# One learning step of a memory layer, reordered: half of a projection held back, slopes, statistics and a halving moved

## The chip, the core and the metric

The program runs on one core of one Trainium2 chip, as one launch. The metric is device time in microseconds (us) of that core; lower is better. The engines are named as in the profile: PE is TensorE (PEld its weight loads), DVE VectorE, ACT ScalarE, POOL GpSimd, SP SyncE, which here only issues DMAs. Each engine runs its own instructions in program order and waits on semaphores for the others.

## What is computed

A two-layer block: a test-time memory and a feed-forward part on layer 0, then attention and a routed mixture of experts on layer 1. The change touches only the first part of the first, the learning of the memory on x (16 sequences of 512 positions, width 128, layer-normalised). It is cut into 8 chunks of 64 positions, and the chunks are learned one after the other:

```
k = rmsnorm(silu(xc @ wk.T), k_norm);  v = silu(xc @ wv.T)
def mem_fwd((w0, w1, ln), k):                      # w0: 256x128, w1: 128x256, ln: 128
    return k + rmsnorm(silu(k @ w0.T) @ w1.T, ln)
def step((mem, surp), (k_c, v_c, th_c, eta_c, beta_c)):
    grads = grad(mean((v_c - mem_fwd(mem, k_c)) ** 2 * th_c))
    clip  = min(1 / (norm(grads) + 1e-6), 1)
    surp  = eta_c * surp - grads * clip
    mem   = beta_c * mem + surp
```

The gates th, eta and beta (1 - alpha) come from sums over the normalised x of the same chunk. Each step needs the memory that the step before it left.

## The kernel before, in words

`learn` holds the learning. A chunk is 1024 rows of 128, that is 8 tiles (`CT`) of 128 x 128, worked on in two halves of 4 tiles (`HT`), h = 0 and h = 1. Every engine has a hand-written list of calls for each step s in 0 to 7; there is no scheduler. The order in the lists and the semaphores alone decide what runs when.

In step s the memory's own work is: PE `hidden` (k @ w0, L437), ACT its tanh (`m_tz`, L629), DVE the silu product (`m_hid`, L858), PE `transpose_h` (L451), ACT `copy_ht` (L637), PE `output` (L461), ACT the squares (L645) and DVE their sums (L868), POOL a power (`m_r`, L768), ACT `normalise_y` (`m_nrm`, L651), and then, for each half, DVE `errors` (L874, L876), `derivatives` (L881 to L890) and `remainder` (L895). `derivatives` contains the dot product over the row (`m_dot`, L888) and its scaled form `m_dr` (L889), for which ACT's `along_y` (L657) waits; `remainder` subtracts what `along_y` wrote and gives `m_dy`. PE transposes `m_dy` (`transpose_dy`, L469), ACT copies it (`copy_dyt`, L667), PE makes the gradients: `grad_hidden` (L478), `grad_w1` (L491), `grad_ln` (L487, which reads `m_en`) and `grad_w0` (L498, after DVE's `grad_hidden`, L904). `norm` (L505 to L508) and DVE's `update` (L908 to L918) end the step.

`slope` (DVE, L862) is the factor tanh - 1 times hidden - 2 that DVE's `grad_hidden` reads. `keep_surprise` (ACT, L663) scales the old surprise; DVE's `decayed` (L899) reads it.

Between these stands work on later chunks. For s + 1: `weigh_keys`, `gates`, `transpose_k` (L406), `copy_kt` (L611), `halve_v` (ACT, L598: v times 0.5), `subtract_v` (POOL). For s + 2: `project` (PE, L397: 4 tiles times wk and 4 times wv for each half, h = 1 first; half 0 waits for `copy_kt`), `project_tanh` (ACT, L587), `silu` (DVE, L836), `square_k` (ACT, L592), `scale_k` (ACT, L603), `sum_products` (L847). For s + 3: `normalise_x` (ACT, L567), transposes and copies of x. For s + 4: `statistics` (DVE, L825 and L830). SP loads a chunk of x (`m_xin`, L352) into the buffer that `normalise_x` of two chunks before has done with. Where no such chunk is left (steps 6 and 7 have no s + 2) the calls drop out.

## Time and profile before

| | |
|---|---|
| time, median of 3 runs | 3584.17 us (3581.29 to 3584.71) |
| the profiled execution: its own time, its span | 3609.93 us, 3608.1 us |
| prologue of the learning | 0 to 51.6 us of the span |
| steps 0 to 7 and what closes the stage | 51.6 to 383.2 us |
| everything behind it, untouched by the change | 383.2 to 3608.1 us |
| busy in the span: PE, DVE, ACT, POOL | 90%, 71%, 58%, 23% |

A step is counted from the start of PE's `hidden` (L437). In step 2 that is 134.34 us of the span, in step 3 175.31 us. Since steps 1 to 4 repeat each other to within 0.01 us, one of them is enough to read.

### The profile page before, as it was taken

To read this page: it belongs to the slowest core of one execution; us is meant where nothing else is said; L and a number is where in the kernel's file an instruction comes from. 1 tells how busy PE (TensorE), PEld (TensorE's weight loads), DVE (VectorE), ACT (ScalarE), POOL (GpSimd) and SP (SyncE) were. 2 spreads that over 40 slices of the span, in tenths; PEclk is the share of its full clock that TensorE was granted. 3 is DMA by queue.
4 is the path that set the end of the run, shared out by engine and by line. 5 is a ranking of instruction groups with operands and counts; after the bars stand their busy time and mean duration, and the time that the engine had idled before them with its cause. 6 is when DMAs were issued, how large, how long until landed. Compare 5 with 4: busy or idle time off the path is not lost. (4 is left out here: it accounts for less than half of the span.)

```text
span 3608.1 us, 77385 instructions
## 1 busy us (share of the span) xinstructions
PE 3255.2 (90%) x30347; PEld 1894.3 (53%) x30347; DVE 2575.5 (71%) x5104; ACT 2079.1 (58%) x4212; POOL 838.7 (23%) x753
## 2 busy tenths in 40 slices
PE   6887599999999699999999999769999999999998
PEld 5776322222222277777777777535555444444454
DVE  5776688888888266676666776577777777777774
ACT  6664177777777544434334333226667776777766
POOL 3331111101110132422423323133333121112110
PEclk8998699999999899999999999879999999999999
DMA  4100211111110000110110110032222112111101
GB/s 137 30 13 1 54 51 49 42 54 46 54 51 28 27 18 28 32 34 22 32 34 22 32 34 22 28 82 57 59 59 49 50 50 67 38 47 42 54 26 29
DMA packets 180473, 151.89 MB, mean 42 GB/s; under 512 B 44388, under 2 KB 160900, under 8 KB 179972
## 3 DMA queue, kind: packets, MB, share of 16 engines
q1 hardware_dynamic: 172228, 140.43, 13.8%
q0 software_dynamic: 6144, 4.72, 1.0%
q8 instruction: 257, 4.21, 0.5%
q10 hardware_dynamic: 1728, 1.57, 0.2%
q14 instruction: 116, 0.95, 0.1%
HBM read 48.45 MB, written 32.65 MB: 22 GB/s over the span
## 5 line engine op out<-in xcount | busy, mean ns | idle before, releaser
L1395 DVE TENSOR_REDUCE b_maxima<-psum 128x2 f32<-128x1024 f32 (+3 forms) x768 | 774.2, 1044 | 236.9 <-PE psum L1227 209.8
L1333 ACT ACTIVATE b_prob<-psum 128x512 f32<-128x512 f32 (+2 forms) x1536 | 725.5, 526 | 332.6 <-PE psum L1260 313.1
L1395 DVE TENSOR_REDUCE c_maxima<-psum 128x2 f32<-128x1024 f32 x512 | 602.6, 1221 | 119.3 <-PE psum L1221 118.2
L1333 ACT ACTIVATE c_prob<-psum 128x512 f32<-128x512 f32 x1024 | 535.9, 602 | 186.7 <-PE psum L1253 186.3
L1860 PEld LDWEIGHTS psum<-consts_layer,a_hid 128*128 128x128 f32 x4096 | 476.2, 192 | 53.6 <-issue 53.3
L1860 PE MATMUL psum<-consts_layer,a_hid 128*128 128x128 f32 x4096 | 477.8, 274 | 0.0
L1850 PE MATMUL psum<-a_x1t,consts_layer 128*128 128x512 f32 x1024 | 461.2, 596 | 11.6 <-issue 11.3
L1917 ACT ACTIVATE a_hid<-psum,consts_layer 128x512 f32<-128x512 f32 x512 | 347.9, 687 | 208.0 <-PE psum L1850 201.1
L1253 PE MATMUL psum<-b_qa,b_ka 64*128 64x512 bf16 (+3 forms) x2048 | 365.5, 303 | 60.8 <-ACT b_prob L1333 56.6
L1275 PE MATMUL psum<-b_prob,b_v 128*32 128x512 f32 (+3 forms) x4096 | 386.8, 450 | 0.3
L2062 DVE SCALAR_TENSOR_TENSOR a_acc<-psum,a_gprob,a_acc 128x128 f32<-128x128 f32 x512 | 143.8, 343 | 266.7 <-PE psum L1860 253.4
L1253 PE MATMUL psum<-c_qa,c_ka 64*128 64x512 bf16 x1024 | 271.0, 382 | 63.9 <-ACT c_prob L1333 62.4
L1221 PE MATMUL psum<-b_ka,b_qa 62*128 62x512 bf16 (+3 forms) x2048 | 300.1, 307 | 27.3 <-DMA b_ka<-b_part 13.2
L1850 PEld LDWEIGHTS psum<-a_x1t,consts_layer 128*128 128x128 f32 x1024 | 187.9, 191 | 213.1 <-issue 204.2
L1253 PEld LDWEIGHTS psum<-b_qa,b_ka 64*128 64x128 bf16 x2048 | 123.0, 93 | 297.5 <-ACT b_prob L1333 223.9
L1275 PE MATMUL psum<-c_prob,c_v 128*32 128x512 f32 x2048 | 272.7, 605 | 0.1
L1260 PE MATMUL psum<-b_kmask,b_pick 64*128 64x64 bf16 x4096 | 253.0, 191 | 0.0
L1221 PE MATMUL psum<-c_ka,c_qa 62*128 62x512 bf16 x1024 | 202.0, 392 | 27.4 <-DMA c_ka<-c_part 13.8
L1227 PE MATMUL psum<-b_qmask,b_pick 64*128 64x64 bf16 x4096 | 221.1, 191 | 3.3 <-issue 3.3
L1227 PEld LDWEIGHTS psum<-b_qmask,b_pick 64*128 64x128 bf16 x4096 | 194.4, 97 | 54.4 <-issue 7.3
L1260 PEld LDWEIGHTS psum<-b_kmask,b_pick 64*128 64x128 bf16 x4096 | 184.8, 95 | 47.3 <-issue 1.7
L1946 POOL TENSOR_TENSOR a_share<-a_gprob,consts_layer 128x512 f32<-128x512 f32 x128 | 134.1, 1048 | 273.2 <-DVE a_gprob L2001 264.4
(343 smaller groups left out, 4303.2 us busy)
## 6 DMA issues: line engine op xcount, KB each, us to landing
b_qa<-b_part SPq DMA_DIRECT2D x192, 128.0 KB
c_qa<-c_part SPq DMA_DIRECT2D x96, 128.0 KB, 2.5
c_ka<-c_part SPq DMA_DIRECT2D x90, 128.0 KB, 2.5
b_ka<-b_part SPq DMA_DIRECT2D x90, 128.0 KB
consts_layer<-layer_in SPq DMA_DIRECT2D x1, 5419.0 KB, 19.2
m_xin<-x SPq DMA_DIRECT2D x16, 256.0 KB, 4.2
xnt<-m_xt SPq DMA_DIRECT2D x16, 256.0 KB, 2.7
c_xt<-xnt SPq DMA_DIRECT2D x16, 256.0 KB, 2.8
```

Of the source, the lines that this page charges most:

```text
L1221: last = nc.tensor.matmul(out[:, half, k0:k0 + w], qa[rows, hh, t * P:(t + 1) * P], ka[rows, hh, 0:w], start=True, stop=not self.causal)
L1227: last = nc.tensor.matmul(out[:, half, k1:k1 + HALF], self.pick[n][rows, :], self.qmask[rows, :], start=False, stop=n == 1)
L1253: last = nc.tensor.matmul(outs[half][:, k0:k0 + w], ka[rows, hh, t * P:(t + 1) * P], qa[rows, hh, q0:S], start=True, stop=not self.causal)
L1260: last = nc.tensor.matmul(outs[half][:, k0 + n * HALF:k0 + (n + 1) * HALF], self.pick[n][rows, :], self.kmask[rows, :], start=False, stop= ...
L1275: last = nc.tensor.matmul(self.acc[32 * j:32 * (j + 1), q0:S], self.values(p)[:, t, column:column + 32], self.prob[:, s % 2, j, q0:S], sta ...
L1333: self.nc.scalar.activation(out, src, ACT.Exp, scale=SCALE).then_inc(self.s.free, 1)
L1395: self.nc.vector.reduce_max(out, src, X).then_inc(self.m.free, 1)
L1850: nc.tensor.matmul(bank[4 + u % 3], K("up0", e * F0 + f * P, P), x1t[n][:, :], start=True, stop=True).then_inc(up_ready.sem, 1)
L1860: last = nc.tensor.matmul(tiled(2 + e % 2)[:, t, :], hid[:, e % 2, f, t * P:(t + 1) * P], K("down0", (e * FC + f) * D, D), start=f == 0, s ...
L1917: nc.scalar.activation(hid[:, e % 2, f, :], bank[4 + u % 3], ACT.Relu, bias=K("upb0", u, 1)).then_inc(hid_ready.sem, 1)
L1946: own.done(nc.gpsimd.tensor_tensor(share[k % 2][:, :, :], along(gprob[n][:, :, k], D), over(K("downb0", k * D, D), T), ALU.mult))
L2062: last = nc.vector.scalar_tensor_tensor(acc[n][:, t, :], tiled(2 + e % 2)[:, t, :], gprob[n][:, t, e:e + 1], acc[n][:, t, :], ALU.mult, AL ...
```

## The change

On PE, `project(s + 2)` is split. Its half 1 stays where it was; its half 0 goes behind `grad_ln(s, 0)` and waits for `m_dr` of half 0. `grad_w1(s, 0)` goes ahead of `grad_hidden(s, 0)`. On DVE, `remainder(s, 0)` goes ahead of `errors(s, 1)`; `slope` leaves the sums of squares: half 0 goes ahead of them, half 1 to between the two halves of `grad_hidden`; `sum_products` goes behind both; `statistics` is cut in two, `sums` (8 BN_STATS) at the head of the step and `moments` (8 BN_AGGR) behind `gates`. On ACT, `halve_v` is gone: the 128 x 128 weight wv is halved once, at the very start (`halve_wv`), and `project_tanh` takes v with scale 1.0; `copy_kt` goes ahead of `normalise_y(s, 1)`, `keep_surprise` behind `along_y(s, 0)`, `square_k(s + 2, 1)` ahead of `along_y(s, 1)`, `normalise_x` is in one piece behind `copy_dyt(s, 1)`, and `scale_k` is in two halves around `copy_xs` and `gate_tanh`. POOL's `subtract_v` waits for `silu` where it waited for `halve_v`.

```diff
@@ project, on PE
                     for h in halves:
+                        pe.wait_ge(wv_halved.sem, 1)
                         pe.wait_ge(xt_copied.sem, xt_copied.at(n, h + 1))
@@ the step's list on PE
                     if has(s + 2):
-                        project(s + 2)
+                        project(s + 2, (1,))
                     grad_ln(s, 0)
+                    if has(s + 2):
+
+                        pe.wait_ge(dr_ready.sem, dr_ready.at(s, 1))
+                        project(s + 2, (0,))
                     transpose_dy(s, 0)
+                    grad_w1(s, 0)
                     grad_hidden(s, 0)
-                    grad_w1(s, 0)
                     grad_ln(s, 1)
@@ new on ACT in place of halve_v
-                def halve_v(n):
-                    act.wait_ge(silu_ready.sem, silu_ready.at(n, 4))
-                    nc.scalar.activation(tv[n % 2][:, :, :], tv[n % 2][:, :, :], ACT.Copy, scale=0.5).then_inc(vn_ready.sem, 1)
+                def halve_wv():
+                    act.wait_ge(consts, 32)
+                    nc.scalar.activation(K("wv"), K("wv"), ACT.Copy, scale=0.5).then_inc(wv_halved.sem, 1)
@@ the step's list on ACT
                     normalise_y(s, 0)
-                    keep_surprise(s)
-                    normalise_y(s, 1)
                     if has(s + 1):
                         copy_kt(s + 1)
+                    normalise_y(s, 1)
                     if has(s + 2):
                         project_tanh(s + 2, (1,))
                     along_y(s, 0)
+                    keep_surprise(s)
                     if has(s + 2):
                         project_tanh(s + 2, (0,))
                     copy_dyt(s, 0)
-                    if has(s + 3):
-                        normalise_x(s + 3, (0,))
-                    if has(s + 1):
-                        halve_v(s + 1)
+                    if has(s + 2):
+                        square_k(s + 2, 1)
                     along_y(s, 1)
                     copy_dyt(s, 1)
                     if has(s + 3):
-                        normalise_x(s + 3, (1,))
+                        normalise_x(s + 3)
                     if has(s + 2):
-                        square_k(s + 2, 1)
                         square_k(s + 2, 0)
@@ the step's list on DVE
+                    if has(s + 4):
+                        sums(s + 4)
                     for h in range(2):
                         hidden(s, h)
                     if has(s + 1):
                         weigh_keys(s + 1)
                         gates(s + 1)
+                    if has(s + 4):
+                        moments(s + 4)
+                    slope(s, 0)
                     output_deviations(s)
                     errors(s, 0)
                     derivatives(s, 0)
                     if has(s + 2):
                         silu(s + 2, 1)
+                    remainder(s, 0)
                     errors(s, 1)
-                    remainder(s, 0)
                     derivatives(s, 1)
                     decayed(s)
                     remainder(s, 1)
                     if has(s + 2):
                         silu(s + 2, 0)
                     grad_hidden(s, 0)
+                    slope(s, 1)
+                    grad_hidden(s, 1)
                     if has(s + 2):
                         sum_products(s + 2)
-                    grad_hidden(s, 1)
-                    if has(s + 4):
-                        statistics(s + 4)
                     update(s)
```

PE's queue in one step, between the transposes of the keys and `grad_w0`, before the change (m_xt is the projection, m_en `grad_ln`, m_dy with m_hid `grad_w1`, m_dyt `grad_hidden`):

```order
L406 MATMUL psum<-consts_shared,m_kn 128x128 x8
L397 MATMUL psum<-consts_memory,m_xt 128x128 x16
L487 MATMUL psum<-m_en,m_ths 128x128 x4
L469 MATMUL psum<-consts_shared,m_dy 128x128 x4
L478 MATMUL psum<-mem,m_dyt 128x256 x4
L491 MATMUL psum<-m_hid,m_dy 128x256 x4
L487 MATMUL psum<-m_en,m_ths 128x128 x4
L469 MATMUL psum<-consts_shared,m_dy 128x128 x4
```

The same place with the change:

```order
L407 MATMUL psum<-consts_shared,m_kn 128x128 x8
L398 MATMUL psum<-consts_memory,m_xt 128x128 x8
L488 MATMUL psum<-m_en,m_ths 128x128 x4
L398 MATMUL psum<-consts_memory,m_xt 128x128 x8
L470 MATMUL psum<-consts_shared,m_dy 128x128 x4
L492 MATMUL psum<-m_hid,m_dy 128x256 x4
L479 MATMUL psum<-mem,m_dyt 128x256 x4
L488 MATMUL psum<-m_en,m_ths 128x128 x4
```

Eight of the sixteen projection products now stand directly ahead of the transposes of the first `m_dy`, and `grad_w1` ahead of `grad_hidden`. DVE's queue behind the first `derivatives`, before (m_tk, m_tv are `silu`, m_m `errors`, m_dy `remainder`):

```order
L890 TENSOR_TENSOR m_dn<-m_dn,m_rth 128x512
L836 SCALAR_TENSOR_TENSOR m_tk<-m_tk,psum 128x512
L836 SCALAR_TENSOR_TENSOR m_tv<-m_tv,psum 128x512
L874 TENSOR_TENSOR m_m<-m_nrm,mem 128x512
L876 TENSOR_TENSOR m_m<-m_m,m_kv 128x512
L895 TENSOR_TENSOR m_dy<-m_dn,m_p 128x512
L881 TENSOR_TENSOR m_en<-m_m,m_nrm 128x512
```

And with the change:

```order
L897 TENSOR_TENSOR m_dn<-m_dn,m_rth 128x512
L844 SCALAR_TENSOR_TENSOR m_tk<-m_tk,psum 128x512
L844 SCALAR_TENSOR_TENSOR m_tv<-m_tv,psum 128x512
L902 TENSOR_TENSOR m_dy<-m_dn,m_p 128x512
L881 TENSOR_TENSOR m_m<-m_nrm,mem 128x512
L883 TENSOR_TENSOR m_m<-m_m,m_kv 128x512
L888 TENSOR_TENSOR m_en<-m_m,m_nrm 128x512
```

The first `m_dy` comes two instructions earlier; everything from L888 on stands at the same count. ACT's queue from the first `copy_dyt` to the second, before (m_tk, m_tv ahead of it are `project_tanh`):

```order
L587 ACTIVATE m_tv<-psum 128x512
L667 ACTIVATE m_dyt<-psum 128x512
L567 ACTIVATE m_xn<-m_xin,m_shift,m_rstd 128x128 x4
L598 ACTIVATE m_tv<-m_tv 128x1024
L657 ACTIVATE m_p<-m_nrm,m_dr 128x128 x4
```

And with the change:

```order
L589 ACTIVATE m_tv<-psum 128x512
L671 ACTIVATE m_dyt<-psum 128x512
L594 ACTIVATE m_sq,m_ks<-m_tk 128x128 x4
L661 ACTIVATE m_p<-m_nrm,m_dr 128x128 x4
L671 ACTIVATE m_dyt<-psum 128x512
L570 ACTIVATE m_xn<-m_xin,m_shift,m_rstd 128x128 x8
```

Ahead of the second `along_y` four squares stand where four normalisations and the halving stood.

## Rows read from the trace of the kernel before

**Rows 1.** Behind the learning: length, PE, PEld, DVE, ACT, POOL busy, clock, DMA, GB/s

```profile
383.20:3608.10 3224.90, 2963.86 (x28649) 1633.74 (x28649) 2329.05 (x4582) 1850.40 (x3578) 731.91 (x651) 0.97 0.16 42
```

**Rows 2.** The same view of steps 0 and 2

```profile
51.63:93.36 41.73, 34.07 (x212) 30.46 (x213) 30.75 (x74) 27.69 (x77) 12.36 (x12) 0.92 0.09 21
...
134.34:175.31 40.97, 34.99 (x215) 31.45 (x214) 30.56 (x66) 28.20 (x80) 13.28 (x12) 0.92 0.11 27
```

**Rows 3.** Timeline of step 2, PE and PEld: start, duration, line, idle before, releaser

```profile
141.51 3.71 PEld L461 LDWEIGHTS psum<-memw1t,m_ht 128*128 128x128 f32 x32 [0.22 <-ACT m_ht L637]
...
146.12 1.95 PE L397 MATMUL psum<-consts_memory,m_xt 128*128 128x128 f32 x16
...
151.30 3.16 PE L397 MATMUL psum<-consts_memory,m_xt 128*128 128x128 f32 x16 [3.23 <-ACT m_kt L611]
...
156.84 0.66 PE L469 MATMUL psum<-consts_shared,m_dy 128*128 128x128 f32 x4 [0.99 <-DVE m_dy L895]
...
158.18 3.23 PE L478 MATMUL psum<-mem,m_dyt 128*128 128x256 f32 x8 [0.69 <-ACT m_dyt L667]
...
163.42 1.05 PE L487 MATMUL psum<-m_en,m_ths 128*128 128x128 f32 x8
...
164.31 0.60 PE L469 MATMUL psum<-consts_shared,m_dy 128*128 128x128 f32 x4
...
164.75 1.89 PE L491 MATMUL psum<-m_hid,m_dy 128*128 128x256 f32 x8
...
166.48 1.89 PE L478 MATMUL psum<-mem,m_dyt 128*128 128x256 f32 x8
...
175.31 3.70 PE L437 MATMUL psum<-mem,m_kt 128*128 128x256 f32 x16
```

**Rows 4.** Timeline of step 2, DVE

```profile
138.02 2.35 DVE L858 SCALAR_TENSOR_TENSOR m_hid<-m_tz,psum 128x1024 f32<-128x1024 f32 x2 [2.67 <-ACT m_tz L629]
...
148.47 0.69 DVE L874 TENSOR_TENSOR m_m<-m_nrm,mem 128x512 f32<-128x512 f32 x1 [1.27 <-ACT m_nrm L651]
...
152.65 0.16 DVE L889 TENSOR_TENSOR m_dr<-m_dot,m_rth 128x4 f32<-128x4 f32 x1
...
154.65 0.68 DVE L874 TENSOR_TENSOR m_m<-m_nrm,mem 128x512 f32<-128x512 f32 x1
...
156.09 0.69 DVE L895 TENSOR_TENSOR m_dy<-m_dn,m_p 128x512 f32<-128x512 f32 x1
...
159.41 0.16 DVE L889 TENSOR_TENSOR m_dr<-m_dot,m_rth 128x4 f32<-128x4 f32 x1
...
160.22 0.89 DVE L899 SCALAR_TENSOR_TENSOR m_base<-mem,m_eb,m_keep 128x640 f32<-128x640 f32 x1
...
161.80 0.69 DVE L895 TENSOR_TENSOR m_dy<-m_dn,m_p 128x512 f32<-128x512 f32 x1 [0.70 <-ACT m_p L657]
...
169.54 1.64 DVE L825 BATCH_NORM_STATS2 m_stats<-m_xin 128x6 f32<-128x128 f32 x8
```

**Rows 5.** Timeline of step 2, ACT

```profile
136.98 2.12 ACT L629 ACTIVATE m_tz<-psum 128x1024 f32<-128x1024 f32 x2
...
159.56 1.04 ACT L598 ACTIVATE m_tv<-m_tv 128x1024 f32<-128x1024 f32 x1
```

**Rows 6.** PE in four stretches of step 2: length, busy, granted clock (1.00 is full speed)

```profile
138.04:141.51 3.47, 2.40 (x20) 1.00 0.00 0
151.95:155.35 3.40, 3.40 (x19) 0.50 0.00 0
155.35:158.75 3.40, 1.73 (x11) 1.00 0.00 0
158.75:162.15 3.40, 3.40 (x10) 0.50 0.02 5
```

**Rows 7.** Timeline of step 6, ACT, without a projection

```profile
317.69 1.28 ACT L657 ACTIVATE m_p<-m_nrm,m_dr 128x128 f32<-128x128 f32 x4 [1.69 <-DVE m_dr L889]
```

**Rows 8.** Loads of x (L352), all 16: issue to landing

```profile
DMA to landing us min/median/max: 3.6/4.2/8.4
```

More of the change, by code:

```diff
@@ L557, in _, with normalise_x @@
             def _(act):
-                def normalise_x(n, halves=(0, 1)):
-                    if 0 in halves:
-                        act.wait_ge(rstd_ready.sem, rstd_ready.at(n, 1))
-                    if 0 in halves and n > 0:
+                def normalise_x(n):
+                    act.wait_ge(rstd_ready.sem, rstd_ready.at(n, 1))
+                    if n > 0:
                         act.wait_ge(xt_ready.sem, xt_ready.at(n, 0))
@@ L564, in normalise_x @@
                         act.wait_ge(prod_ready.sem, prod_ready.at(n - 1, 1))
[L565 to L569 removed]
+                    for t in range(CT):
+                        last = nc.scalar.activation(xn[:, t, :], xin[n % 2][:, t, :], ACT.Identity, bias=shift[:, t:t + 1], scale=rstd[:, t:t + 1])
+                    last.then_inc(xn_ready.sem, 1)
                 def copy_xt(n, h):
@@ L687, in _ @@
                     square_k(0, h)
-                halve_v(0)
                 for h in range(2):
@@ L739, in _ @@
                             copy_xt(s + 3, h)
+                    if has(s + 2):
+                        scale_k(s + 2, (0,))
+                    if has(s + 3):
                         copy_xs(s + 3)
@@ L742, in _ @@
                         gate_tanh(s + 2)
-                        scale_k(s + 2)
+                        scale_k(s + 2, (1,))
                 copy_w1t(NC)
@@ L826, in statistics, with moments @@
                     own.done(last)
+                def moments(n):
                     if n > 0:
```

39 lines of the change are left out of this document (21 added, 18 removed).

## The prediction

> **What bounds the kernel now.** First the windows by stage: 3224.9 us of the span lie behind the learning [rows 1], and no line of the change is there; whatever it brings must come out of the eight steps. The windows by step show that a step takes 40.97 us with PE busy for 34.99 us, and that the mean granted clock is 0.92 [rows 2]. No engine is full, so I read one step, step 2, engine by engine in the timeline, and looked in each for the wait that ends last.
>
> PE's rows [rows 3] are read from the end. From the transposes of the second `m_dy` (L469) at 164.31 us to the next step's `hidden` at 175.31 us PE's list runs through without a wait that matters: 11.00 us, a tail of fixed length. Ahead of it PE has also been busy since 158.18 us. The last real waits are 0.69 us for `copy_dyt` at 158.18 us and 0.99 us for the first `m_dy` at 156.84 us. So the step is as long as the first `m_dy` is late, plus what PE has queued behind it. That queue is also slower than it need be. `grad_hidden` and `grad_w1`, 8 rows each, take 5.24 us together (158.18 to 163.42), where at full clock each takes 1.73 us (164.75 to 166.48). The windows say why: the granted clock is 0.50, that is 1.2 GHz in place of 2.4, from 151.95 to 155.35 us and again from 158.75 to 162.15 us, each time behind a stretch in which PE had waited, with 3.23 us of idle before 151.30 us and with 1.73 us of work in 3.40 before the second [rows 3, 6].
>
> DVE's rows [rows 4] show the other chain. DVE has no wait between 148.47 us, the first `errors`, and 161.1 us, the end of `decayed`; then it waits 0.70 us for ACT's `along_y`, which ACT could start only behind `halve_v`, at 160.60 us [rows 5], though `m_dr` had been ready since 159.57 us. The second `m_dy` is done at 162.49 us. PE reaches its transposes only at 164.31 us, so today PE's queue decides, by 1.8 us.
>
> **The change, part by part, in the times of step 2.**
>
> *Head of the step.* The tanh of the first half starts at 136.98 us [rows 5], while half of the 3.70 us of `hidden` after 134.34 us is done by about 136.3 us: ACT was in `scale_k`. Half of `scale_k` now comes before `copy_xs`, in time in which ACT waited for PE, so the tanh comes about 0.6 us sooner. PE however has the transposes of the other half to do first; what reaches `output` is the 0.22 us for which it waited for `copy_ht` [rows 3]. I take 0.2 us, and move all later times by it. The 8 BN_STATS, 1.64 us, now stand ahead of DVE's `hidden`. DVE waited there for 2.67 us, 2.1 us with the earlier tanh [rows 4]; they fit with 0.45 us over, and cost nothing as long as their x has landed (third rival). The aggregates and `slope` of half 0 fall where DVE waited for squares of y. Leaving the tail they save nothing, since DVE waited for `norm` anyway. The halving of wv is one 128 x 128 operation, hidden under the first load and POOL's powers: nothing.
>
> *First `m_dy`.* `remainder` goes ahead of two `errors` operations of 0.72 us. It may start when the silu products end, 154.65 - 0.2 = 154.45 us; its `along_y` has started at `m_dr` (152.81 - 0.2 + 0.1) and takes 1.28 us [rows 7], so it is ready at 154.0 us. `m_dy` is done at 155.15 us, where it was 156.78 us: 1.6 us sooner.
>
> *The held half.* It starts at `m_dr`, about 152.7 us. Where it stood before, it had 151.30 to 154.46 us; it takes 1.95 us at full clock (146.12 us) and 3.16 us at half [rows 3]. It is on PE's path now, since it stands ahead of the transposes. Behind it PE has the transposes (164.31 to 164.75, 0.44 us), `grad_w1` and `grad_hidden` (1.73 us each) and `grad_ln` (163.42 to 164.31, 0.89 us), with no wait, as `grad_w1` needs no copy and gives `copy_dyt` its time. 152.7 + 1.95 + 0.44 + 1.73 + 1.73 + 0.89 = 159.45 us at full clock. A half-speed stretch of 3.4 us, as both in rows 6 are, adds 1.7 us: one gives 161.15 us, two that lie wholly on this piece 162.85 us. I expect one always, because PE still idles for some 2.5 us before the first `grad_ln`, and part of a second now and then.
>
> *Second `m_dy`.* DVE's count of instructions to it is the same, so 161.1 - 0.2 = 160.9 us for the end of `decayed`. `along_y` can start at 159.57 - 0.2 = 159.4 us: ahead of it now stand four squares, which are done before, and ends at 160.75 us. The wait of 0.70 us is gone; `m_dy` is done at 160.9 + 0.69 = 161.6 us, its transposes can start at 161.65 us.
>
> *Sum of a step.* The tail starts at the later of PE's and DVE's times: 161.65 us with up to one half-speed stretch, 162.85 us with two, against 164.31 us. Gains of 2.66 and 1.46 us; I take 2.3 us, nearer to DVE's end, because the second stretch rarely lies wholly there. What is late next is DVE. The tail stays 11.00 us if ACT keeps up: `copy_dyt`, the whole normalisation of x, four squares and the squares of the gradients come to 6.5 us there, and `grad_w0` ends 7.5 us after the tail's start. `slope` of half 1, 1.2 us, lies where DVE waits for PE's second `grad_hidden`. Cover gone, it would cost those 1.2 us.
>
> *All steps.* Six steps (0 to 5) have a projection: 6 x 2.3 = 13.8 us. Step 0 was 41.73 us long, 0.76 us more than step 2 [rows 2], which I take to be more slow PE work in the same piece, gone with it: 0.8 us more. Steps 6 and 7 have no silu products to cover `along_y`: DVE waits about 0.7 us in front of `remainder`, but still gives the first `m_dy` 1.44 - 0.7 = 0.7 us sooner, and PE is what counts there: 0.7 us each, 1.4 us. Together 16.0 us. The profiled execution took 3609.93 us, 0.7% above the median of the runs; the terms are the same few microseconds in either: 3609.93 - 16.0 = 3593.9 us, and 3584.17 - 16.0 = 3568.2 us.
>
> **Rivals.**
>
> *The clock gives it back.* The split leaves PE one more gap, between the first `grad_ln` and the held half, and a wait of up to 1.2 us for the second `m_dy`. If each step gets two full half-speed stretches or a new one in the tail, its gain is 1.2 to 1.46 us. For it: today each step has two. Against it: from 152.7 us on PE has work nearly without a break. 6 x 1.3 + 0.8 + 0 = 8.6 us: 3575.6 us.
> The Trainium skill ("TensorE: Matmul & The Clock Gate", "A second HAM failure mode") says that short idles between groups of matmuls can make the clock go back and forth between its two levels; by that rule this case holds. Its "Part 4: PE-mode transpose" says that transposes do not count as busy in the same way, which would make the first `m_dy`'s transposes a gap too. The trace does not bear that out: between 138.04 and 141.51 us PE did hardly anything but transposes of `m_hid`, and the clock stayed at 1.00 [rows 6].
>
> *A queue on ACT eats most of it.* The second tanh of the held half stands ahead of `copy_dyt`, four squares and the second `along_y`. With the projection at half clock its last tanh ends at 156.5 us, `copy_dyt` at 157.3 us, the squares at 158.5 us; `along_y` is due at 159.4 us. If the 0.9 us of room is not there and 1.3 us more are lost on top, a gain of 1 us a step is left: 3578 us, about the edge of no change.
>
> *Slower, by the load of x.* BN_STATS stands at the head of DVE's queue, with the silu products of the hidden layer behind it, PE's transposes behind them, and so the whole step. Its x is loaded into the buffer that `normalise_x` frees, and this now ends in one piece at about 166.3 us. With 1.3 us for two issues and 4.2 us to land it is there at 171.8 us, some 2.1 us before DVE asks for it. The longest load took 8.4 us [rows 8]: late by 2.1 us, of which 0.45 us is covered. It turns a step's gain into a loss above 4.2 + 2.1 + 0.45 + 2.3 = 9 us. Were loads to take 11 us, each of steps 0 to 3 would lose 2 us and the rest gain little: about 3592 us. No load in the trace took so long.
>
> **How the numbers follow.** Forecast 0.61, the clock 0.20, ACT's queue 0.13, the load 0.06. 0.2% of this kernel is 7.2 us, about what a measurement can tell from no change. The first two are faster by more than that, and a little of the third: 0.83; same 0.12; slower 0.05. The best that the bounds allow is 6 x 2.66 + 0.8 + 2 x 1.4 (the 0.69 us before `grad_hidden` also gone in steps 6 and 7) = 19.6 us, 3564.6 us; less the runs' own spread of some 3 us, and as much again for a clock that comes out better, 3560 us. The upper end takes in the clock's case and ends at ACT's: 3578 us.
>
> **What would show it.** In the changed profile: steps of some 38.7 us; the first `m_dy` about 20.8 us after `hidden`, the second about 27.3 us; DVE without a wait before the second `remainder`; PE without one between the held half and `grad_ln`, then at most a short one for the second `m_dy`; mean clock of a step above 0.92. I am wrong if DVE waits for x at BN_STATS, if the distance from the second transposes to the next `hidden` is more than 11.0 us, or if PE shows two stretches at 0.50 between the held half and them.

## The result and the profile after

| | before | after |
|---|---|---|
| time, median (lowest to highest) | 3584.44 us (3581.29 to 3585.27), 4 runs | 3556.83 us (3555.72 to 3559.12), 4 runs |
| ratio, 95% interval | | 0.9925 (0.9908 to 0.9943) |
| profiled execution: own time, span | 3609.93 us, 3608.1 us | 3559.12 us, 3557.3 us |
| start of step 0, end of the last w1 transposes | 51.63, 381.88 us | 50.62, 353.43 us |

The change takes 27.6 us off, where 16.0 were forecast: the right direction, and a gain 1.7 times as large. The two profiled spans lie 50.8 us apart. Only 28.45 us of that are in the learning. The other 22.35 us lie behind it, in work that is the same in both kernels (3226.22 and 3203.87 us). That part belongs to the execution that was profiled, which for the kernel before took 25 us more than the median. In the later profiles it took 3220 to 3225 us on one chip and 3198 to 3207 us on two others, with the change or without it. So only the learning is compared here.

The windows by step of the changed kernel, each from the start of `hidden` (now L438) to the next; the first is the prologue. Columns as in [rows 2]:

```profile
0.00:50.62 50.62, 24.72 (x152) 23.96 (x153) 18.46 (x70) 28.11 (x90) 20.48 (x28) 0.87 0.76 233
50.62:87.75 37.13, 31.59 (x213) 28.62 (x213) 30.62 (x75) 28.03 (x80) 11.32 (x12) 1.00 0.10 24
...
124.88:162.01 37.13, 31.60 (x214) 28.62 (x214) 30.40 (x66) 27.46 (x79) 12.24 (x12) 1.00 0.12 29
...
199.15:236.99 37.84, 34.14 (x215) 31.28 (x214) 28.41 (x50) 27.70 (x79) 12.23 (x12) 0.91 0.06 15
236.99:274.23 37.24, 31.68 (x191) 28.79 (x190) 28.01 (x49) 24.67 (x74) 10.15 (x8) 0.90 0.03 7
274.23:313.34 39.11, 30.03 (x153) 26.03 (x153) 25.04 (x45) 16.25 (x37) 4.93 (x4) 0.83 0.00 0
313.34:353.43 40.09, 28.33 (x145) 24.80 (x145) 24.64 (x44) 15.39 (x35) 2.58 (x3) 0.81 0.00 1
```

Steps were 41.73, 40.98, 40.97, 40.97, 40.97, 40.52, 41.33 and 42.78 us long and are now 37.13, 37.13, 37.13, 37.14, 37.84, 37.24, 39.11 and 40.09 us: 27.4 us less in all. In steps 0 to 3 the mean granted clock is 1.00; it was 0.92 [rows 2]. PE's busy time fell with it, 34.99 to 31.60 us, for the same products (215 and 214 records). DVE's busy time is what it was (30.56 and 30.40 us).

It is tempting to stop at that clock: the steps became short when the half-speed stretches went. But step 4 is at clock 0.91, with 34.14 us of busy PE, and is only 0.7 us longer than step 3. So a slow clock as such does not make a step 3.8 us longer; it depends on what the slow stretch lies on, as the experiments show. PE in step 2, in the timeline, from the projection to the second `m_dy`:

```profile
136.33 1.95 PE L398 MATMUL psum<-consts_memory,m_xt 128*128 128x128 f32 x16
139.88 1.16 PE L488 MATMUL psum<-m_en,m_ths 128*128 128x128 f32 x8 [1.60 <-DVE m_en L888]
142.07 2.05 PE L398 MATMUL psum<-consts_memory,m_xt 128*128 128x128 f32 x16 [1.04 <-DVE m_dr L896]
144.60 0.66 PE L470 MATMUL psum<-consts_shared,m_dy 128*128 128x128 f32 x4 [0.47 <-DVE m_dy L902]
145.09 1.89 PE L492 MATMUL psum<-m_hid,m_dy 128*128 128x256 f32 x8
146.82 1.89 PE L479 MATMUL psum<-mem,m_dyt 128*128 128x256 f32 x8
148.54 1.05 PE L488 MATMUL psum<-m_en,m_ths 128*128 128x128 f32 x8
150.96 0.66 PE L470 MATMUL psum<-consts_shared,m_dy 128*128 128x128 f32 x4 [1.36 <-DVE m_dy L902]
```

Every wait that is left is for DVE, the last of them 1.36 us long. Before, PE came to the second transposes without a wait [rows 3]. The bound has gone over to DVE's chain, and what counts is when that chain starts and how long it is. Its start, in the rows of POOL, ACT and DVE of the same step. POOL's `m_r` is the inverse root with which y is normalised, a power over 128 x 4 elements, once for each half:

```profile
135.22 0.17 DVE L876 TENSOR_SCALAR m_ss<-m_ss 128x4 f32<-128x4 f32 x1
135.47 1.01 POOL L772 TENSOR_TENSOR m_r<-m_ss,m_power 128x4 f32<-128x4 f32 x1 [4.80 <-DVE m_ss L876]
136.51 1.14 ACT L655 ACTIVATE m_nrm<-psum,m_r 128x128 f32<-128x128 f32 x4 [0.26 <-POOL m_r L772]
137.68 0.69 DVE L881 TENSOR_TENSOR m_m<-m_nrm,mem 128x512 f32<-128x512 f32 x1 [0.51 <-ACT m_nrm L655]
...
150.22 0.68 DVE L902 TENSOR_TENSOR m_dy<-m_dn,m_p 128x512 f32<-128x512 f32 x1
```

The same place in the kernel before:

```profile
144.95 0.17 DVE L869 TENSOR_SCALAR m_ss<-m_ss 128x4 f32<-128x4 f32 x1
145.17 1.22 DVE L862 SCALAR_TENSOR_TENSOR m_dz<-m_tz,m_dz 128x1024 f32<-128x1024 f32 x1
145.20 3.08 POOL L768 TENSOR_TENSOR m_r<-m_ss,m_power 128x4 f32<-128x4 f32 x2 [5.08 <-DVE m_ss L869]
```

And the source line's view of POOL's power over all 16 instructions, before and then after (shortest, median and longest in ns):

```profile
L768 POOL TENSOR_TENSOR m_r<-m_ss,m_power x16: 1006/1508/2079, 62.2 to 353.4; 128x4 f32<-128x4 f32 x16
```

```profile
L772 POOL TENSOR_TENSOR m_r<-m_ss,m_power x16: 1006/1009/1019, 61.2 to 327.4; 128x4 f32<-128x4 f32 x16
```

Before, two powers in a row took 3.08 us: 2.08 and 1.01. Now each takes 1.01 us. It is the first of each step that has become 1.07 us shorter, and in the kernel before DVE ran `slope` of half 1 beside it, 1.22 us, which reads two operands in SBUF. The change moved that `slope`. The first `errors` starts 12.80 us after `hidden` (137.68 - 124.88), where it started 14.13 us after it (148.47 - 134.34, [rows 4]), and DVE has no wait from there to the second `m_dy`. Of the 1.33 us, 1.07 are the power; the other 0.26 were there before it, since the first sum of squares ends about that much earlier after `hidden`, close to the 0.2 us that the prediction took for the earlier tanh.

### The profile page after: what moved, and what is told of

Its sections match the earlier page's. It is cut to its first block and busy times, and to the rows that moved or that the text cites. A ratio compares the mean times of both kernels' runs of the same rounds, so it can differ in the third digit from the quotient of the medians.

```text
span 3557.3 us, 77385 instructions
## 1 busy us (share of the span) xinstructions
PE 3228.3 (91%) x30347; PEld 1876.0 (53%) x30347; DVE 2573.2 (72%) x5104; ACT 2074.8 (58%) x4205; POOL 830.2 (23%) x753
## 5 line engine op out<-in xcount | busy, mean ns | idle before, releaser
L1236 PE MATMUL psum<-c_ka,c_qa 62*128 62x512 bf16 x1024 | 201.2, 391 | 27.4 <-DMA c_ka<-c_part 13.6
```

The costliest lines, as they stand in the source:

```text
L1236: last = nc.tensor.matmul(out[:, half, k0:k0 + w], qa[rows, hh, t * P:(t + 1) * P], ka[rows, hh, 0:w], start=True, stop=not self.causal)
```

## The experiments

Three theories of the part that the prediction missed. The lock (L in the expectations): a DVE operation with two inputs in SBUF holds up POOL's power beside it, and moving it away starts DVE's chain 1.07 us sooner in each of the eight steps. The clock: the steps became shorter since PE no longer drops to half speed, which the held half of the projection brings. The order: `remainder` and `grad_w1` put forward bring more than the sum gave them. The times of the kernel before differed between the chips (3605.68 us for the first four kernels, 3584.36 for the next four, 3584.03 for the last four), so each kernel is given as a ratio to the kernel before beside it. Steps are those of the profiled execution, steps 0 to 7.

**`slope` of half 1 moved alone, in the kernel before.**

```diff
                     for h in range(2):
-                        slope(s, h)
+                        if h == 0:
+                            slope(s, 0)
                         dve.wait_ge(y_squared ...
...
+                    slope(s, 1)
                     grad_hidden(s, 1)
```

> The kernel before with one edit: slope of half 1 leaves the place between the two sums of squares and goes between the two grad_hidden of DVE. Theory L (POOL's power of half 0 is held while DVE's slope, with both inputs in SBUF, runs beside it): the first power takes 1.0 us in place of 2.08 us, and since the first m_dy comes 1.1 us sooner and PE decides, every step is 1.1 us shorter: 8.5 us in all, 3576 us. Rival C (only the clock and the order on PE brought the time): the power's length is an artefact of the trace, the step stays at 40.97 us, 3584 us.

Ratio 0.9990 (0.9980 to 1.0000), 3602.57 us. POOL's first power fell to 1.01 us as expected, the time hardly at all. The ten runs lie between 3590.69 and 3608.79 us, and the profiled one, with 3594.41 us, is among the fastest. Its steps are 39.45, 38.83, 39.71, 38.81, 39.70, 37.79, 39.97 and 42.23 us long, with one half-speed stretch ahead of the second `m_dy` in each of steps 0 to 5, where steps 1 to 5 of the kernel before have two: 16.8 us after `hidden` in the shorter ones and 22.3 us in the longer. In both kinds the first `m_dy` comes 1.06 us earlier after `hidden` and PE reaches the second transposes without a wait, so in this execution PE's queue decides, and steps 1 to 4 are 2.2 and 1.3 us shorter. The median moved by 3.1 us of the 8.5 that were expected, the interval reaches from 0 to 7 us, and no trace shows what took the rest in the other nine runs. The move of `slope` alone is worth little; whether it is worth something behind the other edits is the next kernel's question.

**`slope` of half 1 put back, in the changed kernel.**

```diff
                     for h in range(2):
+                        if h == 1:
+                            slope(s, 1)
                         dve.wait_ge(y_squared ...
...
                     grad_hidden(s, 0)
-                    slope(s, 1)
                     grad_hidden(s, 1)
```

> The changed kernel with slope of half 1 put back between the two sums of squares. Theory L: first power back to 2.1 us, first normalisation 1.1 us later, DVE's chain to the second m_dy with it: steps of 38.2 us in place of 37.13 us, 9 us in all, 3566 us. Rival C: less than 2 us, 3558 us. If PE's later start also brings a stretch at half clock back, up to 1.7 us more in some steps: up to 3573 us.

Ratio 0.9943 (0.9927 to 0.9960), 3585.92 us. At the changed kernel's ratio it would be 0.9925 x 3605.68 = 3578.6 us, so putting it back costs 7.3 us, with intervals that overlap. The next kernel, which has `slope` in its new place and the time of the changed kernel, ran on the same chip: all its runs (3575.55 to 3580.19 us) lie below all of these (3581.95 to 3592.39), 8.5 us in the medians. The profile is sharper. POOL's power, and the first `errors` of step 1:

```profile
L772 POOL TENSOR_TENSOR m_r<-m_ss,m_power x16: 1006/1508/2077, 63.5 to 335.5; 128x4 f32<-128x4 f32 x16
...
105.00 0.69 DVE L883 TENSOR_TENSOR m_m<-m_nrm,mem 128x512 f32<-128x512 f32 x1 [1.28 <-ACT m_nrm L655]
```

The same 2.08 us as in the kernel before, and `errors` starts 13.86 us after `hidden` (105.00 - 91.14) in place of 12.80. The steps are 39.88, 38.21, 38.85, 38.21, 38.21, 37.75, 39.00 and 41.29 us. Steps 1 and 3 are 38.21 - 37.13 = 1.08 us and 1.07 us longer: the power's 1.07 us. All eight together are 8.6 us longer, but not by 1.08 us each: step 0, with a half-speed stretch on `hidden`, is 2.75 us longer, step 4 is 0.37 us longer and step 6 0.1 us shorter, as the half-speed stretches fall otherwise in the two profiles. That the sum is eight times the power's price is partly luck. The price itself is shown.

**The projection not held: whole, at its old place.**

```diff
-                        project(s + 2, (1,))
+                        project(s + 2)
                     grad_ln(s, 0)
-                    if has(s + 2):
-                        pe.wait_ge(dr_ready.sem, dr_ready.at(s, 1))
-                        project(s + 2, (0,))
```

> The changed kernel with the whole projection in its old place, behind copy_kt, and without the wait for m_dr. PE then works through both halves and the first grad_ln and has some 3 us of nothing before the first m_dy. Theory C (the hold pays by keeping PE busy, and the clock up, in front of the gradients): granted clock 0.50 in a stretch behind that gap in steps 0 to 5; where it falls on grad_w1 and grad_hidden they end about 1.8 us later, of which the wait of 1.4 us for the second m_dy covers most: 0.4 us a step, 3559 to 3562 us, with the mean clock of a step near 0.92. Rival (the hold pays by its order): no drop of the clock and no change, 3557 us.

Ratio 0.9923 (0.9906 to 0.9939), 3577.41 us: that of the changed kernel. The steps are 38.75, 37.15, 37.16, 37.24, 37.24, 36.80, 38.19 and 39.64 us. Each of steps 1 to 5 has a half-speed stretch now. Step 0, step 2 and the stretch in step 2, in the windows:

```profile
51.58:90.33 38.75, 32.91 (x212) 29.71 (x213) 30.62 (x74) 28.14 (x80) 11.30 (x12) 0.96 0.10 23
...
127.48:164.64 37.16, 32.69 (x215) 29.80 (x214) 30.44 (x66) 27.48 (x79) 12.24 (x12) 0.95 0.12 29
147.00:150.40 3.40, 3.19 (x10) 2.75 (x11) 3.33 (x7) 2.38 (x11) 0.00 (x0) 0.50 0.02 5
```

In step 2 the clock is 0.95 against 1.00, PE is busy for 1.1 us more, and the step is as long as in the changed kernel to 0.03 us. The stretch lies on `grad_w1`, and the 1.37 us for which PE otherwise waits for the second `m_dy` cover it. Step 0 shows the other case. Its stretch lies at the very start, on `hidden`, which takes 5.31 us in place of 3.70, and the step is 1.6 us longer: there nothing covers it. The holding of the projection, the edit by which the change is named, keeps the clock up in steps 1 to 3 and brings nothing here that the time shows. The clock theory falls for steps 1 to 5, not for every place in a step.

**PE kept busy in the kernel before.** `fill(n)` is n products of the identity with itself, 128 x 128, whose result nobody reads; nothing is left out.

```diff
-                        project(s + 2)
+                        project(s + 2, (1,))
+                        fill(10)
+                        project(s + 2, (0,))
                     grad_ln(s, 0)
+                        fill(3)
                     transpose_dy(s, 0)
+                        fill(2)
                     grad_hidden(s, 0)
```

> The kernel before with idle time of PE filled: 10 products of 128 x 128 with no use before the second half of the projection, 3 behind the first grad_ln, 2 behind the transposes of the first m_dy, in steps 0 to 5. Theory C: the granted clock stays at 1.00, grad_hidden and grad_w1 take 3.5 us in place of 5.24 us, a step is 1.8 us shorter: 10.7 us in all, 3573.5 us. Rival: the filling itself delays what stands behind it by as much as the clock gives, 3584 us.

Ratio 0.9991 (0.9982 to 1.0001), steps 1 to 4 of 40.65 to 40.92 us. The filling took away the first half-speed stretch and left the second, 23.2 to 27.2 us after `hidden`, ahead of the second `m_dy`. So it did not make the kernel that it was meant to make. It says only that without the first stretch, and with the filling, steps 1 to 4 are 0.05 to 0.33 us shorter.

**`remainder(s, 0)` back behind `errors(s, 1)`, in the changed kernel.**

```diff
-                    remainder(s, 0)
                     errors(s, 1)
+                    remainder(s, 0)
```

> The changed kernel with the first remainder back behind the second errors. The first m_dy comes 1.4 us later, DVE's count of instructions to the second is the same. Theory D (since the power is free of the lock, DVE's chain to the second m_dy sets the step, and PE has room of about 1.3 us before it): at full clock PE is ready at 150.9 us of step 2 where DVE's m_dy is due at 150.96 us, so the step stays at 37.2 us; where a stretch at half clock falls on this piece it is up to 1.7 us longer. Total 3 to 8 us over the changed kernel, which by its ratio is 3578.6 us on this chip: 3580 to 3587 us. Rival P (PE's queue from the first m_dy still sets the step): 1.4 us in every step, 11 us, 3590 us.

Ratio 0.9961 (0.9947 to 0.9975), 3569.63 us; 12.2 us slower than the changed kernel at its ratio. That is more than the 3 to 8 us expected and near the rival's 11. The profiled execution, with 3562.86 us the fastest of the five, does not bear out the rival's way, 1.4 us in every step; its steps are 38.68, 37.16, 38.69, 37.15, 37.16, 36.70, 38.00 and 40.26 us. Two windows, of a short and of a long one:

```profile
89.20:126.36 37.16, 32.88 (x214) 29.87 (x214) 30.43 (x66) 27.62 (x79) 12.28 (x12) 0.95 0.12 29
126.36:165.05 38.69, 33.06 (x214) 29.79 (x214) 30.16 (x65) 27.51 (x79) 12.25 (x12) 0.96 0.12 28
```

Both have one half-speed stretch, and the clock's mean is if anything better in the long step. It is the place that differs: 17.6 to 21.1 us after `hidden` in the short one, on the held half of the projection, where it comes out of PE's wait for the first `m_dy` (0.57 us of 1.93 are left), and 21.5 to 24.9 us in the long one, on `grad_w1` itself. In the timeline of the long one PE waits 1.93 us for that `m_dy` and then takes 3.38 us for what took 1.89:

```profile
147.54 0.89 PE L470 MATMUL psum<-consts_shared,m_dy 128*128 128x128 f32 x4 [1.93 <-DVE m_dy L902]
148.22 3.38 PE L492 MATMUL psum<-m_hid,m_dy 128*128 128x256 f32 x8
```

What the early `remainder` buys is room on PE: 1.36 us of wait for the second `m_dy`, into which such a stretch can fall. With the late one that room is gone (PE comes to the second transposes at 154.06 us in this step, without a wait), and a stretch behind the first `m_dy` lengthens the step by 1.5 us. Eight such steps would make the 12.2 us, but the profiled learning is only 1.0 us longer than the changed kernel's (303.80 and 302.81 us). That the slower four runs have more long steps is argued, not shown.

**`grad_hidden` ahead of `grad_w1` again, in the changed kernel.**

```diff
                     transpose_dy(s, 0)
-                    grad_w1(s, 0)
                     grad_hidden(s, 0)
+                    grad_w1(s, 0)
```

> The changed kernel with grad_hidden ahead of grad_w1 for the first half, as before the change, so that PE waits about 0.9 us for copy_dyt. Theory D: within PE's room, step 37.13 us unchanged at full clock, at most 3 us in all, 3579 to 3582 us. Rival P: 0.7 to 0.9 us a step, 6 us, 3585 us.

Ratio 0.9938 (0.9921 to 0.9955), 3559.86 us, steps of 37.04 to 37.45 us up to step 5 and 40.35 and 42.27 us in the last two, which were 39.11 and 40.09. In step 1 PE's wait for the second `m_dy` is 0.42 us where it was 1.36: the old order uses up room on PE and takes no time there. At the changed kernel's ratio it would be 3557.5 us: a difference of 2.4 us, which the intervals do not tell from none.

**`halve_v` back on ACT ahead of `along_y(s, 1)` and in the prologue.** The computation is that of the changed kernel, with v instead of wv halved.

```diff
                         square_k(s + 2, 1)
+                    if has(s + 1):
+                        halve_v(s + 1)
                     along_y(s, 1)
```

> The changed kernel with halve_v back: in the prologue behind the squares, in each step ahead of the second along_y (1.04 us on ACT); wv is copied onto itself with scale 1.0. In the step ACT has waited there for m_dr for 1.8 us, so the halving is free: steps of 37.13 us. In the prologue I expect the 1.0 us back by which the first hidden comes sooner with the change (50.62 for 51.63 us). In all 1 us, 3579.6 us. Rival (ACT's queue ahead of along_y is what the removal of halve_v freed): 0.7 us a step and more, 3584 us.

Ratio 0.9921 (0.9904 to 0.9939), 3555.70 us: no difference. Steps 0 to 3 are 37.14, 37.14, 37.72 and 37.15 us. Behind the squares and a halving of 1.05 us ACT still waits 0.83 us for `m_dr` before `along_y` (step 1). Step 0 starts at 51.81 us, where it started at 50.62 us; the last kernel below shows what that is worth.

**Three kinds of DVE operation beside POOL's power.** In the changed kernel DVE gets one more operation at the place that `slope` had: in steps 0 and 4 a product of two tiles in SBUF, in 1 and 5 a sum over one tile, in 2 and 6 a copy of one tile, in 3 and 7 nothing. The results are not read. The kernel ran once, 3564.89 us, and only its trace is used.

```diff
+                    if s % 4 == 0:
+                        nc.vector.tensor_tensor(scr[:, :, :], tz[:, part(0), :], tz[:, part(1), :], ALU.mult)
+                    elif s % 4 == 1:
+                        nc.vector.tensor_reduce(scs[:, :], tz[:, part(1), :], X, ALU.add)
+                    elif s % 4 == 2:
+                        nc.vector.tensor_copy(scr[:, :, :], tz[:, part(1), :])
```

> The changed kernel with an extra operation of DVE, whose result nobody reads, in the old place of slope of half 1, beside POOL's first power: in steps 0 and 4 a product of two SBUF inputs (1.2 us), in 1 and 5 a sum over one SBUF input, in 2 and 6 a copy of one SBUF input, in 3 and 7 none. The length of POOL's first power tells what holds it. Theory L (two inputs in SBUF hold it): 2.1 us in steps 0 and 4, 1.0 us in the others. Rival A (any long operation of DVE on SBUF does): 2.0 us in 1 and 5 too. Rival B (the power is longer for another reason, such as its own place behind slope): 1.0 us everywhere.

POOL's power in steps 0, 1, 2 and 3, and in the first three DVE's operation beside it, in the timeline:

```profile
62.18 1.22 DVE L876 TENSOR_TENSOR m_scr<-m_tz 128x1024 f32<-128x1024 f32 x1
62.35 2.93 POOL L774 TENSOR_TENSOR m_r<-m_ss,m_power 128x4 f32<-128x4 f32 x2 [5.88 <-DVE m_ss L888]
...
100.23 1.22 DVE L878 TENSOR_REDUCE m_scs<-m_tz 128x4 f32<-128x1024 f32 x1
100.40 1.01 POOL L774 TENSOR_TENSOR m_r<-m_ss,m_power 128x4 f32<-128x4 f32 x1 [4.80 <-DVE m_ss L888]
...
137.38 0.69 DVE L880 COPY m_scr<-m_tz 128x1024 f32<-128x1024 f32 x1
137.55 1.38 POOL L774 TENSOR_TENSOR m_r<-m_ss,m_power 128x4 f32<-128x4 f32 x1 [4.80 <-DVE m_ss L888]
...
175.07 1.01 POOL L774 TENSOR_TENSOR m_r<-m_ss,m_power 128x4 f32<-128x4 f32 x1 [4.54 <-DVE m_ss L888]
```

Of the same length, 1.22 us, the operation with two inputs adds 0.91 us to the first power (2.93 less the second's 1.01 is 1.92) and the one with one input nothing. So it is not that DVE is busy, nor that both read SBUF. The copy, with one input, adds 0.37 us, which no theory on record had. The ends say how the hold works: the power is done 0.87 us behind the end of the product (62.35 + 1.92 against 62.18 + 1.22), 0.86 us behind the end of the copy (138.93 against 138.07) and, in the kernel before, 0.89 us behind the end of `slope` (147.28 against 146.39). It gets on only when DVE's operation is over, whatever that one's length. The steps follow: 38.03, 37.16, 37.51 and 37.15 us, that is 0.90, 0.03, 0.38 and 0.02 more than 37.13. Steps 0 and 2 also have a half-speed stretch, but the time is lost ahead of it: the first `errors` starts 13.69, 12.81, 13.17 and 12.80 us after `hidden`. Steps 4 to 7, with the same four kinds, show the powers again (1.91, 1.02, 1.32 and 1.01 us). The Trainium skill ("SBUF — State Buffer", "🔬 SBUF: two separate sides") says that VectorE and GpSimd share a port pair under an exclusive lock, which a VectorE operation takes with two SBUF inputs or in a 2-port mode, and that a plain fp32 copy from SBUF to SBUF runs in that mode; the loser waits for the whole instruction. This case's rows agree on all three operations: 0.91, 0 and 0.37 us.

**The two swaps alone, in the kernel before.**

```diff
+                    remainder(s, 0)
                     errors(s, 1)
-                    remainder(s, 0)
...
+                    grad_w1(s, 0)
                     grad_hidden(s, 0)
-                    grad_w1(s, 0)
```

> The kernel before with two swaps and nothing else: the first remainder ahead of the second errors on DVE, and grad_w1 ahead of grad_hidden on PE for the first half. Theory P then D: PE gets from the first m_dy to its second transposes 1.4 us + 0.7 us sooner and stops deciding; DVE's chain, with the power still held by slope, decides: second transposes about 27.4 us after hidden, or 28.1 us if the wait for halve_v stays, steps of 38.4 to 39.1 us in place of 40.97 us. Over the stage 13 to 18 us less than before: a ratio of 0.995 to 0.9965. Rival (without the hold PE stays late, since the projection and the first grad_ln run at half clock in front of the first m_dy): steps above 40 us, less than 6 us.

Ratio 0.9956 (0.9938 to 0.9975), 3565.88 us. Steps of 38.20, 38.47, 38.47, 38.47, 38.47, 38.02, 39.67 and 40.63 us, steps 1 to 4 2.50 us shorter than before. Steps 1, 2 and 4 have a half-speed stretch, step 3 has none, and they are equally long: DVE decides. Two swapped pairs of calls bring 18.2 us, of the 26.3 that the whole change brings on the same chip (3584.03 to 3557.71 us), with the projection whole, `halve_v` in place and POOL's power still at 2.08 us:

```profile
138.34 3.09 POOL L768 TENSOR_TENSOR m_r<-m_ss,m_power 128x4 f32<-128x4 f32 x2 [5.08 <-DVE m_ss L869]
```

**The swaps and `slope`.** As the kernel before this one, with `slope` of half 1 between the two `grad_hidden`, behind `sum_products`, which stays there.

> The two swaps, and slope of half 1 moved as in the changed kernel; everything else as before (projection in one piece, statistics in the tail, halve_v, old queue of ACT). If the two swaps and the free power are the change, steps are 37.3 us (37.13 us and the 0.2 us of the tanh behind scale_k), the stage ends within 3 us of the changed kernel's, ratio 0.993. If the hold or the queue of ACT carries a part of its own, they are 38 us or more, ratio 0.995.

Ratio 0.9939 (0.9919 to 0.9959), 3560.99 us. POOL's powers take 1.01 us, and the transposes of the second `m_dy` start 26.35 us after `hidden` (154.33 - 127.98). But the steps are 38.03 us long, not 37.3: the tail has grown to 11.66 us. By the expectation's own rule 38 us would point to the hold or ACT's queue; the trace points elsewhere. The timeline of DVE and PE from these transposes on:

```profile
154.33 0.66 PE L469 MATMUL psum<-consts_shared,m_dy 128*128 128x128 f32 x4 [1.36 <-DVE m_dy L896]
...
155.39 1.21 DVE L905 SCALAR_TENSOR_TENSOR m_dz<-m_dz,psum 128x1024 f32<-128x1024 f32 x1
156.53 1.48 DVE L847 TENSOR_REDUCE m_R<-m_prod 128x10 f32<-128x1280 f32 x1
157.92 1.21 DVE L862 SCALAR_TENSOR_TENSOR m_dz<-m_tz,m_dz 128x1024 f32<-128x1024 f32 x1
159.24 1.22 DVE L905 SCALAR_TENSOR_TENSOR m_dz<-m_dz,psum 128x1024 f32<-128x1024 f32 x1
...
160.51 1.78 PE L498 MATMUL psum<-m_dz,m_kn 128*128 128x256 f32 x7 [0.34 <-DVE m_dz L905]
```

With both `sum_products` (1.48 us) and `slope` (1.21 us) ahead of the second `grad_hidden` DVE is late for `grad_w0`. The change moves `sum_products` behind it, and its tail is 11.05 us. That edit cost and brought nothing in the prediction; behind the other two it is worth about 0.6 us a step by this trace. No kernel moves it alone. The other 0.27 us of a step (26.35 for 26.08) are the head's: the first `errors` starts 13.08 us after `hidden` in place of 12.80.

**PE filled everywhere.** The changed kernel with products as in the fourth experiment in all of PE's gaps up to the second `m_dy`, and, in the two steps without a projection, `remainder(s, 0)` between the two operations of `errors(s, 1)`, where it does not wait for `along_y`.

```diff
+                    fill(5 if has(s + 2) else 12)
                     grad_ln(s, 0)
+                    fill(3 if has(s + 2) else 7)
...
                     grad_ln(s, 1)
+                    fill(4)
                     transpose_dy(s, 1)
...
+                    if s in (5, 6):
+                        fill(6, 0)
...
-                    remainder(s, 0)
-                    errors(s, 1)
+                    if has(s + 2):
+                        remainder(s, 0)
+                        errors(s, 1)
+                    else:
+                        errors(s, 1, lambda: remainder(s, 0))
```

> The changed kernel with PE's idle time filled by products with no use (5 before the first grad_ln, 3 before the held half, 4 before the second transposes in steps 0 to 5; 12, 7 and 4 in steps 6 and 7; 6 behind the end of steps 5 and 6), and in steps 6 and 7 the first remainder between the two operations of the second errors. If idle time brings the half clock: granted clock 1.00 in all steps, steps 4 and 5 at 37.1 and 36.6 us, 6 and 7 at 37.5 and 38.0 us, some 5 us less than the changed kernel: ratio 0.991. Rival (the filling delays as much as it gives, or the clock falls all the same): 0.9925 or worse.

Ratio 0.9913 (0.9893 to 0.9932), 3552.35 us (3550.07 to 3554.28): the fastest of all, 5.4 us below the changed kernel on the same chip. Its windows, of step 2 and of the last two:

```profile
126.05:163.18 37.13, 34.28 (x239) 31.30 (x238) 30.40 (x66) 27.49 (x79) 12.24 (x12) 1.00 0.12 29
...
274.16:309.79 35.63, 31.35 (x210) 28.55 (x211) 25.82 (x45) 16.27 (x37) 4.93 (x4) 1.00 0.00 1
309.79:347.06 37.27, 29.04 (x191) 26.35 (x191) 24.66 (x44) 15.41 (x35) 2.58 (x3) 1.00 0.00 1
```

Step 2 is as long as without the filling, at the same clock. The last two are 3.5 and 2.8 us shorter than in the first profile of the changed kernel (2.4 and 3.5 than in the second), with the clock at 1.00 where it was 0.83 and 0.81. There the clock does count: in step 6 the first `errors` starts 1.44 us sooner after `hidden`, where the changed kernel has a stretch on `hidden`, and PE needs 2.04 us less from the first transposes to the second (5.74 for 7.78), which it reaches without a wait in both kernels. The filling and the moved `remainder` (0.81 us of wait for `along_y`) were not run apart. The 1.44 us lie ahead of the moved call, so they are not its doing; of the 2.04 it may hold a part.

**The changed kernel once more.**

> The changed kernel as it is, beside the others on their chip, with a second profile. The step is DVE's chain, so the steps without a stretch at half clock are 37.13 us again; in which steps such a stretch falls may differ from the first profile, and with it the stage by up to 0.7 us a step. Ratio 0.9925.

Ratio 0.9931 (0.9911 to 0.9951), 3557.71 us. The steps are 37.12, 37.13, 37.14, 37.13, 37.81, 36.68, 38.00 and 40.79 us; step 0 starts at 51.60 us, though the kernel is the one that started it at 50.62 us. So the prologue varies by 1 us from one execution to the next, and the 1.0 us by which it was shorter in the first profile is no gain of the change that these runs can show.

## Why the prediction was wrong in size

*What bounds the kernel.* Right: PE's queue decides in the kernel before. The two swaps show it, which give PE room and take 2.50 us off a step with the power still held. The kernel with `slope` alone moved does not settle it: if PE's queue starts with the first `m_dy`, as the prediction has it, each step should have become 1.07 us shorter, and the median shows 3.1 us in all.

*First and second `m_dy`.* The mechanism was right, and so was the conclusion that DVE is late next. Forecast were transposes 20.8 and 27.3 us after `hidden`; measured are 19.72 (144.60 - 124.88) and 26.08 us. Both come 1.1 to 1.2 us earlier, since the whole chain starts earlier. The sum for PE left out one wait: at full clock the held half is done before the first `m_dy`, and PE waits 0.47 us for it. That decides nothing, since DVE is later still. The tail came out at 11.05 us for the forecast 11.00, by the letter above the 11.0 that it named as a sign of being wrong, and too little to matter.

*The step that failed* is in "Head of the step": "The aggregates and `slope` of half 0 fall where DVE waited for squares of y. Leaving the tail they save nothing". With it the prediction took DVE's start of `errors` as given but for the tanh's 0.2 us. It priced `slope` of half 1 only at the place to which it goes ("Cover gone, it would cost those 1.2 us"); what its leaving the old place gives is put at nothing without a word. It was not nothing: beside it POOL's power took 2.08 us, and ACT and then DVE waited for that. The view of that line says so ahead of any run: of 16 equal instructions the longest takes twice the shortest. Measured: 1.08 us a step by putting it back (steps 1 and 3), 8.6 us over the eight steps of the profile and 7.3 us in the medians. That is most of the 11.6 us between 16.0 and 27.6. The measured gain also lies beyond the 19.6 us that the prediction called the best its bounds allow, so a term was missing and not only a size taken too small.

*The held half and the clock.* A second, smaller miss, of size. The sum took 2.3 us of the bound 2.66 for a second half-speed stretch in part of the steps. Steps 0 to 3 have none at all, and the one in step 4 is two stretches long and costs 0.7 us. Steps 1 to 3 gained 3.84 us: 2.66 as DVE's bound had it, 1.07 by the power, and 0.1 that is left over. The 2.66 - 2.3 = 0.36 us make 2 us over six steps. That the held half is to thank for it is not so: without it steps 1 to 3 are as long. What shows in the clock is a result of PE's order and waits that the time does not depend on in these steps.

*Steps 6 and 7.* 0.7 us each were forecast; they gained 2.22 and 2.69 us. In the two profiles the gain of step 6 falls into three parts. The first `errors` starts 1.24 us sooner after `hidden` (14.30 for 15.54), most of it the power. From there to the transposes of the first `m_dy` it is 0.68 us less, the 0.7 of the forecast, with a wait for `along_y` of 0.81 us where 0.7 was taken. From these to the second transposes it is 0.30 us less. In step 7 the parts are 1.01, 0.67 and 1.01 us. The term that was priced was right, then, and the head was missing here too. How the last part splits between the order on PE and the clock stays open: the same kernel's second profile has 38.00 and 40.79 us for the two steps in place of 39.11 and 40.09.

*The halving.* "Nothing", and nothing it was: with `halve_v` back the time is the same.

*The rivals.* None came. The clock's rival is refuted for this kernel (no stretch in steps 0 to 3), though the fifth experiment shows what it feared, 1.5 us in two steps of its profile, once the early `remainder` is taken back. ACT was never late for the second `along_y`, and in the view of the line of BN_STATS DVE waits for x twice, 6.6 us in all, as it did in the kernel before (6.5 us), and that is the first load at the start of the kernel; in step 2 the eight of them start at 125.80 us, right behind the update.

In sum, in the profiles, steps 0 to 7 together: the two swaps take 19.9 us off (330.25 to 310.40), `slope` on top 3.6 (to 306.83), and the rest of the change, of which only the place of `sum_products` was found as a cause, 4.0 (to 302.81). Taken out of the whole change, `slope` is worth 8.6: the parts do not add up to the same whichever comes first. One reason is in the trace: behind the swaps alone, `slope` and `sum_products` together delay `grad_w0`. These are single profiles, and how the half-speed stretches fell is in each of the sums.

## What to carry to other kernels

Before a move is priced at nothing because its engine waits at the old place, look at what the *other* engines do beside it: where a line's shortest and longest duration differ by a factor of two on equal shapes, look for a neighbour that holds it up. A better clock is no gain in itself. Compare two steps of the same kernel, one with and one without the half-speed stretch; if they are equally long, another engine decides at that place. Elsewhere in the same step such a stretch can cost its full price (1.6 us on `hidden`, 1.5 us behind a late `m_dy`). And an edit worth little alone (`slope` in the kernel before) can be worth 1 us a step behind another that moves the bound, so it is tried again there.

## What the runs showed that I had not expected

A held-up POOL operation shows no wait in the trace, only a longer duration: 2.08 us for a power that takes 1.01 alone, beside a DVE product of two SBUF operands; 1.92 beside another such product of 1.22 us, 1.38 beside a copy of 0.69 us, 1.01 beside a sum over one operand of 1.22 us. It goes the other way as well. In step 6 of the changed kernel `slope` runs beside POOL's product of keys and values and takes 1.60 us, where it takes 1.29 in step 2; in the second profile it takes 2.47 us there:

```profile
302.05 2.36 POOL L791 TENSOR_TENSOR m_kv<-m_kn,m_tv 128x1024 f32<-128x1024 f32 x1 [12.38 <-DVE m_dy L902]
303.02 2.47 DVE L870 SCALAR_TENSOR_TENSOR m_dz<-m_tz,m_dz 128x1024 f32<-128x1024 f32 x1
```

In all three `slope` ends 1.07 to 1.08 us behind the end of POOL's product (here 305.49 against 304.41), however early it started. So the change has moved `slope` from a place where it held POOL up to one where POOL can hold it up; it costs nothing there, because PE's second `grad_hidden` comes later still.

The kernel with `slope` alone moved had ten runs 18 us apart on one chip (3590.69 to 3608.79 us); the changed kernel had runs 3 us apart, four on either of two chips. That the former's spread comes from where the half-speed stretches fall was only argued, from the steps of its one profile.
